# First attention of a two-layer block on one core: value products of two key blocks in halves of the columns, sums and bias on GpSimd

## The reference, cut to what matters

```
q, k, v = h @ Wq.T + bq, h @ Wk.T + bk, h @ Wv.T + bv      # h = layernorm(x), 64 columns each
weights = softmax(q @ k.T / 8, causal)
x = x + (weights @ v) @ Wo.T + bo
```

## Time and profile before

| | |
|---|---|
| median of 3 runs | 2892.86 us (2884.68 to 2895.48) |
| the profiled execution's own time | 2893.18 us |
| its span, first to last instruction | 2891.3 us |
| PE busy | 2605.1 us, 90% |
| DVE busy | 2001.3 us, 69% |
| ACT busy | 1590.3 us, 55% |
| POOL busy | 397.3 us, 14% |
| granted TensorE clock, mean | 0.959 of full speed |

### The profile page before, as it was taken

How to read it: one execution, slowest core, us unless ns; L and a number is a source line. 1 busy time by engine, 2 the same in 40 slices (tenths; PEclk the granted TensorE clock), 3 DMA queues, 4 the chain that set the end, 5 groups by cost and what they waited for, 6 DMA issues and landing times.

```text
span 2891.3 us, 57833 instructions
## 1 busy us (share of the span) xinstructions
PE 2605.1 (90%) x21618; PEld 1170.1 (40%) x21618; DVE 2001.3 (69%) x4383; ACT 1590.3 (55%) x3169; POOL 397.3 (14%) x417
## 2 busy tenths in 40 slices
PE   6798789899899899999899889999989989899996
PEld 3444333334344344443344434343344434334344
DVE  4557778776666777777675677877667577887832
ACT  2324356555545556555564556656555466666663
POOL 2322020201102011120201202020010110000011
PEclk9889799999999999999999999999999999999998
DMA  2423131211311313130221312213031131111101
GB/s 56 135 73 111 45 97 31 75 53 38 87 36 48 97 45 97 31 104 16 75 65 33 97 36 79 71 45 97 23 87 38 40 104 38 45 52 38 33 28 35
DMA packets 238692, 175.93 MB, mean 61 GB/s; under 512 B 88721, under 2 KB 238162, under 8 KB 238418
## 3 DMA queue, kind: packets, MB, share of 16 engines
q1 hardware_dynamic: 236560, 170.39, 20.8%
q10 hardware_dynamic: 1858, 1.84, 0.2%
HBM read 87.17 MB, written 84.41 MB: 59 GB/s over the span
## 4 chain that ended last, share of the span: by engine, by line
PE 57%; DVE 20%; ACT 6%; SPq 6%; issue 4%; DMA 4%; DVEq 1%; POOL 1%; POOLq 0%; ACTq 0%
DVE mx L1273 14%; PE psum L1556 12%; PE psum L1537 10%; PE psum L1510 6%; PE psum L1444 4%; SPq L754 4%; PE psum L1478 4%; ACT probs L1053 3%; DMA rest_dram<-parts 2%; PE psum L1418 2%; PE psum L1360 2%; PE psum L1574 2%; PE psum L1497 2%; DVE stats L1154 2%; PE psum L1584 2%
## 5 line engine op out<-in xcount | busy, mean ns | idle before, releaser
L1273 DVE TENSOR_REDUCE mx<-psum 128x1 f32<-128x512 f32 (+3 forms) x2560 | 1386.9, 601 | 343.5 <-PE psum L1510 169.6
L1053 ACT ACTIVATE probs<-psum 128x512 f32<-128x512 f32 (+3 forms) x2560 | 1186.3, 538 | 710.1 <-PE psum L1537 427.7
L1537 PE MATMUL psum<-qst,kst 34*128 34x512 bf16 (+7 forms) x5120 | 680.9, 353 | 58.1 <-ACT probs L1053 23.2
L1556 PE MATMUL psum<-probs,vs 128*17 128x512 f32 (+3 forms) x5120 | 607.8, 547 | 2.2 <-ACT probs L1053 1.6
L1510 PE MATMUL psum<-kst,qst 64*128 64x512 bf16 (+3 forms) x2560 | 450.4, 357 | 91.5 <-DVE mx L1273 31.1
L1537 PEld LDWEIGHTS psum<-qst,kst 64*128 64x128 bf16 (+1 forms) x5120 | 196.6, 95 | 412.7 <-DVE mx L1273 144.3
L1510 PEld LDWEIGHTS psum<-kst,qst 64*128 64x128 bf16 x2560 | 131.3, 94 | 501.0 <-ACT probs L1053 182.9
L888 POOL TENSOR_SCALAR vare<-mv 128x4 f32<-128x4 f32 x64 | 14.9, 232 | 1615.1 <-DVE mv L1157 1615.1
L1013 ACT ACTIVATE probs<-psum 128x1024 f32<-128x1024 f32 x80 | 74.6, 939 | 141.9 <-PE psum L1424 80.8
L1556 PEld LDWEIGHTS psum<-probs,vs 128*17 128x17 f32 x5120 | 86.3, 96 | 159.7 <-issue 103.8
L1516 PE MATMUL psum<-maskq,identh 64*128 64x128 bf16 x2048 | 147.8, 219 | 0.0
(11 more groups left out here) (150 smaller groups left out, 2584.2 us busy)
## 6 DMA issues: line engine op xcount, KB each, us to landing
main_dram<-parts SPq DMA_DIRECT2D x256, 128.0 KB
rest_dram<-parts SPq DMA_DIRECT2D x128, 128.0 KB
qst<-main_dram SPq DMA_DIRECT2D x128, 128.0 KB, 2.8
kst<-main_dram SPq DMA_DIRECT2D x128, 128.0 KB, 2.8
v_dram<-vst SPq DMA_DIRECT2D x64, 136.0 KB, 4.0
vs<-v_dram SPq DMA_DIRECT2D x64, 136.0 KB, 2.3
xs<-x_in SPq DMA_DIRECT2D x16, 512.0 KB, 4.0
x_dram<-xs SPq DMA_DIRECT2D x16, 512.0 KB, 3.1
```

The source lines that it names most:

```text
L1053: act.activation(probs[:, HG * (step_no(b, hg, k) % 2) + 2 * pair + odd, 0:cols], bank(PLAN.home["scores", item[:4]][odd], 0, cols), ACT.E ...
L1273: dve.tensor_reduce(mx1[:, n % 2, 2 * g + odd, i % TPC, c:c + 1], bank(PLAN.home["max", item[:5]][odd], 0, width(i, c)), AX.X, ALU.max).th ...
L1537: ins = pe.matmul(two[odd][:, 0:CH - off], kst[rows, kslot, part, pair, keys], qst[rows, qslot, part, pair, off:CH], start=(part == 0), st ...
L1556: ins = pe.matmul(bank(7, off, CH, rows=VW, row=32 * h), vtile[:, h, :], probs[:, HG * (step_no(b, hg, k) % 2) + h, 0:CH - off], start=(kb ...
```

## The change

- For q of 1 to 3, `values0` writes the even block of a pair to PSUM rows 0 to 63 and the odd block to rows 64 to 127, so the two use the left and the right half of the array's columns. For q = 0 both blocks go to rows 0 to 63, one after the other as before. The column of ones is gone; v0 has 64 columns. The planner knows it as a new mode "H", at half the time of before for q of 1 to 3.
- `copy0` copies 128 rows (64 for q = 0). `wo0` holds Wo twice, in rows 0 to 63 and 64 to 127, so that `WO0` 1 and 2 add the halves in their contraction.
- A new job `sum0` on GpSimd adds up each pair's exponentials in `sums0` (128 x 512): for a full pair two additions that wait for one another, for the first pair of q of 1 to 3 one addition of the two blocks. `exp0` of pair n now waits for `sum0` of pair n-2 too. `WO0` 0 multiplies `sums0` with a column of ones and waits for the chunk's last `sum0`, not for `copy0`.
- A new job `bias0` on GpSimd adds the bias to x, once for each chunk, after the first norm; `add0` waits for it. The bias (bo, and bv times Wo, spread over all rows with one matmul at the start) is in `boc`.
- At the start, one weight load more on SP's queue, one of 128 KB instead of 1 KB on ACT's, two small memsets and some waits fewer on GpSimd, one small multiplication on DVE.

```diff
-SWITCH = {("F", "R"): 0.31, ...}
+SWITCH = {..., ("F", "H"): 0.31, ("R", "H"): 0.15, ("C", "H"): 0.14, ("H", "C"): 0.14, ("H", "F"): 0.14, ("H", "R"): 0.14}
+    add("POOL", "bias0", c, key(0), 2.4, ("norm", (0, *c)))
...
-        add("ACT", "exp0", (*c, kp), key(0.6), 0.17 + 0.853 * size, ("scores0", (*c, kp)), ("values0", old),
+        add("ACT", "exp0", (*c, kp), key(0.6), 0.17 + 0.853 * size, ("scores0", (*c, kp)), ("values0", old), ("sum0", old),
             free=("scores0", (*c, kp)))
-        add("PE", "values0", (*c, kp), key(0.6), 1.71 * size - (0.21 if diagonal else 0), ("exp0", (*c, kp)),
-            ("v0", (b, 2 * kp // TPC)), ("values0", (*c, kp - 1) if kp else None), lat=0.1, claim="O" if kp == 0 else None, mode="F")
-    add("ACT", "copy0", c, key(), 0.5, ("values0", (*c, pairs - 1)), *[("WO0", p and (*p, n)) for n in range(3)],
+        less = P / CH if diagonal else 0.0
+        add("PE", "values0", (*c, kp), key(0.6), 0.86 * size if q else 0.86 * (2 * size - less), ("exp0", (*c, kp)),
+            ("v0", (b, 2 * kp // TPC)), ("values0", (*c, kp - 1) if kp else None), lat=0.1, claim="O" if kp == 0 else None, mode="H")
+        add("POOL", "sum0", (*c, kp), key(0), 1.2 * (2 * size - less if kp or not q else 1.0), ("exp0", (*c, kp)),
+            ("sum0", (*c, kp - 1) if kp else None), ("WO0", p and kp == 0 and (*p, 0) or None))
+    add("ACT", "copy0", c, key(), 0.5, ("values0", (*c, pairs - 1)), *[("WO0", p and (*p, n)) for n in (1, 2)],
...
-        add("PE", "WO0", (*c, n), key(), 0.3 if n == 0 else 0.86, ("copy0", c), lat=0.1, claim="P", mode="F")
+        add("PE", "WO0", (*c, n), key(), 1.0 if n == 0 else 0.86, ("copy0", c) if n else ("sum0", (*c, pairs - 1)),
+            lat=0.1, claim="P", mode="F")
...
+                elif kind == "bias0":
+                    b, q = item
+                    wt.wait_ge("ready", 1)
+                    wt.job("norm", (0, b, q))
+                    x = xs[:, q % 2, :, :]
+                    pool.tensor_tensor(x, x, boc[:, :].unsqueeze(1).broadcast_to([P, TPC, D]), ALU.add).then_inc(S["bias0"], 1)
+                elif kind == "sum0":
+                    b, q, kp = item
...
+                    if kp == 0 and q:
+                        pool.tensor_tensor(sums0[:, :], even, odd, ALU.add).then_inc(S["sum0"], 1)
+                        continue
+                    links += 1
+                    if kp == 0:
+                        pool.tensor_copy(sums0[:, :], even).then_inc(S["chain s"], 1)
+                    else:
+                        pool.tensor_tensor(sums0[:, off:CH], sums0[:, off:CH], even, ALU.add).then_inc(S["chain s"], 1)
+                    wt.wait_ge("chain s", links)
+                    pool.tensor_tensor(sums0[:, lo:CH], sums0[:, lo:CH], odd, ALU.add).then_inc(S["sum0"], 1)
...
-                        ins = pe.matmul(ps[0:DK0 + 1, lo:CH], v0[:, kb, :], probs0[:, n % 2, odd, lo - off:CH - off],
-                                        start=(kb == 0), stop=(kb == TPC * (q + 1) - 1))
+                        up, first = (odd, kp == 0) if q else (0, kb == 0)
+                        ins = pe.matmul(ps[DK0 * up:DK0 * (up + 1), lo:CH], v0[:, kb, :],
+                                        probs0[:, n % 2, odd, lo - off:CH - off], start=first,
+                                        stop=(kp == TPC * (q + 1) // 2 - 1 if q else kb == TPC - 1))
...
-                            ins = pe.matmul(ps[:, t:t + 1], osb0[:, P * t:P * (t + 1)], wo0[:, D:D + 1],
+                            ins = pe.matmul(ps[:, t:t + 1], sums0[:, P * t:P * (t + 1)], wo0[:, D:D + 1],
```

More of the change, by code:

```diff
@@ L312, in chunk_jobs @@
         else:
-            add("DVE", "add0", (*c, n), key(), 0.79, ("WO0", (*c, n)), ("rec0", c), ("norm", (0, *c)),
+            add("DVE", "add0", (*c, n), key(), 0.79, ("WO0", (*c, n)), ("rec0", c), ("bias0", c),
                 free=("WO0", (*c, n)))
@@ L892, in _ @@
                         pool.memset(kst[:, :, 1, :, :], 1.0).then_inc(done, 1)
+                elif kind == "bias0":
[3 more added lines that the diff above has]
+                    x = xs[:, q % 2, :, :]
+                    pool.tensor_tensor(x, x, boc[:, :].unsqueeze(1).broadcast_to([P, TPC, D]),
+                                       ALU.add).then_inc(S["bias0"], 1)
+                elif kind == "sum0":
+                    b, q, kp = item
+                    old = before(b, q)
+                    n = len(PAIRS0) * b + PAIR_AT[q, kp]
+                    off = span(q, 2 * kp)
+                    lo = span(q, 2 * kp + 1)
+                    even = probs0[:, n % 2, 0, 0:CH - off]
+                    odd = probs0[:, n % 2, 1, lo - off:CH - off]
+                    wt.job("exp0", item)
+                    if kp == 0:
+                        wt.job("WO0", old and (*old, 0))
+                    else:
+                        wt.job("sum0", (b, q, kp - 1))
+                    if kp == 0 and q:
+                        pool.tensor_tensor(sums0[:, :], even, odd, ALU.add).then_inc(S["sum0"], 1)
+                        continue
+                    links += 1
+                    if kp == 0:
+                        pool.tensor_copy(sums0[:, :], even).then_inc(S["chain s"], 1)
+                    else:
+                        pool.tensor_tensor(sums0[:, off:CH], sums0[:, off:CH], even, ALU.add).then_inc(S["chain s"], 1)
+                    wt.wait_ge("chain s", links)
+                    pool.tensor_tensor(sums0[:, lo:CH], sums0[:, lo:CH], odd, ALU.add).then_inc(S["sum0"], 1)
                 elif kind == "bias":
@@ L1010, in _ @@
                         wt.job("values0", (bb, *PAIRS0[m]))
+                        wt.job("sum0", (bb, *PAIRS0[m]))
                     wt.job("scores0", item)
@@ L1017, in _ @@
                     old = before(b, q)
-                    for n in range(3):
+                    for n in (1, 2):
                         wt.job("WO0", old and (*old, n))
                     wt.job("values0", (b, q, TPC * (q + 1) // 2 - 1))
-                    act.activation(osb0[:, :], home("values0", (b, q, 0))[0:DK0 + 1, :], ACT.Copy
+                    rows = slice(0, P if q else DK0)
+                    act.activation(osb0[rows, :], home("values0", (b, q, 0))[rows, :], ACT.Copy
                                    ).then_inc(S["copy0"], 1)
@@ L1217, in _ @@
                         wt.wait_ge("weights", W0)
-                        dve.tensor_tensor(wo0[DK0:DK0 + 1, 0:D], bank(7, 0, D, rows=1, row=DK0),
-                                          wo0[DK0:DK0 + 1, 0:D], ALU.add).then_inc(S["ready"], 1)
+                        dve.tensor_tensor(boc[:, :], bank(7, 0, D), boc[:, :], ALU.add).then_inc(S["ready"], 1)
                         eight_bit_weights()
@@ L1228, in _ @@
                     wt.job("rec0", (b, q))
-                    wt.job("norm", (0, b, q))
+                    wt.job("bias0", (b, q))
                     wt.job("WO0", item)
@@ L1401, in _ @@
                         wt.wait_ge("weights", W0)
-                        pe.matmul(bank(7, 0, D, rows=DK0 + 1), bvcol[:, :], wo0[0:DK0, 0:D], start=True, stop=True
+                        wt.wait_ge("spread", 1)
+                        pe.matmul(bank(7, 0, D), bvcol[:, :], wo0[0:DK0, 0:D], start=True, stop=True
                                   ).then_inc(S["apart"], 1)
```

49 lines of the change are left out of this document (28 added, 21 removed).

## The result

The changed kernel takes 2877.35 us (median of 6 runs, 2870.71 to 2883.92), the kernel before, run beside it, 2893.09 (2884.68 to 2895.48): a ratio of 0.9949 [0.9929, 0.997], 16 us or 0.5% faster. The forecast was 2854 (2832 to 2880). The side was right and the time lies in the range, but less than half of the 39 us came.

The account below looks back on a forecast made before the run. PE was taken as the only limit inside the values0 bursts, with DVE limiting some of what follows. 44 us gained - 3 (modes) - 2 (DVE) = 39, from a median of 2892.86 to 2854 us, range 2832 to 2880.

Parts of the forecast that it names:

- Products, 53 us less: values0 on PE: pairs in halves run together, a full pair falling from 1.86 to 0.98 us; 53 us less PE work.
- the 44 in the sum: Part of the 53 us of PE work expected to reach the end: 35 us in batches 1 to 3, 9 in batch 0.
- 0.88 and 0.7: Shares of saved PE work taken to reach the end: 0.88 in batches 1 to 3, 0.7 in batch 0.
- The rest on PE, ACT: WO0 contracting 128 rows instead of 65, and copy0 with 128 rows: nothing.
- The 3 us for modes: values0 no longer shares a mode with transposes and projections: 3 us lost (0 to 11).
- GpSimd paces the bursts: Rival: sums of 17.8 us against bursts of 18 to 19 us set the pace; 2878 us, chance 0.10.
- the slower rival: PE stands at WO0 0 for a sum0 behind a late root; 2934 or 2918 us, chance 0.06.
- GpSimd's work on the chain, 2 us: DVE standing still while GpSimd writes: DVE's 20% of the chain applied to 10 us, 2 us lost.
- DVE time lost: DVE work such as xn and xrk held up by more GpSimd work: 10 us of DVE time (0 to 20).
- The start, nothing (at most 1 us): One more SP load issue, fewer POOL memsets, a small DVE multiplication: nothing, at most 1 us either way.
- Order, 10 either way: New order on PE, DVE and ACT: may move time by 10 us either way, put only in the range.

Follow-up runs that it names:

- e13: Changed kernel, a pair's value products one after the other and GpSimd's new work left out; ratio 1.0059 to the kernel before; its two theories expected at most 2900 us.
- e3: Changed kernel, same order and waits, GpSimd's new work left out (sums and bias not computed); 2854.19 us, ratio 0.9879 to the kernel before.
- e2: Changed kernel with ACT's weight loads held behind memsets and the first bias0 held until DVE has made the 8-bit weights; 2867.88 us, ratio 0.9929.
- e5: e2 with batch 0's sum0 replaced by a memset of one column; 2861.23 us, ratio 0.9892 to the kernel before.
- e1: Changed kernel with ACT's weight loads issued only behind ten GpSimd memsets, as before the change; 2873.95 us, ratio 0.9949.
- e15: e2 with each addition of batch 0's sums replaced by a GpSimd power of 4 columns: queue nearly as full, hardly any data moved; 2871.19 us, ratio 0.9919.
- e14: e2 with the second chunk's load issued on SP ahead of the later weights; 2862.06 us, ratio 0.9903 to the kernel before.
- e8: Kernel before, with WO0 0 planned at 1.0 us instead of 0.3, only the order changed; 2884.45 us, ratio 0.9968.
- e12: Kernel before, with the plan's LEAD at 84 instead of 85, only the order changed; 2881.83 us, ratio 0.9955.
- e11: Changed kernel, with WO0 0 planned at 0.3 us again instead of 1.0, only the order changed; 2882.34 us, ratio 0.995.
- e4: Changed kernel in its own order, both blocks of every pair to rows 0 to 63, one after the other; 2911.21 us, ratio 1.0077.

## Why the prediction was right in sign and wrong in size

**Products, 53 us less: right.** A pair takes 1.01 us for a forecast 0.98. PE's busy time fell 47 us for a forecast 50. Without GpSimd's work the halves bring 52 us of total time (e13 to e3, some 8 either way; 46 in their traces) for the 44 in the sum. So 0.88 and 0.7 for what reaches the end were not too high; the loss stood elsewhere.

**The rest on PE, ACT: right.** `WO0` and the copies cost nothing: a 128-row copy takes 598 ns, and a matmul of `WO0` 1 or 2 with 128 rows 389 ns for 409. `exp0` waited 2.8 us for sums. The 3 us for modes weren't measured by themselves; they are in what the order costs, below.

**GpSimd paces the bursts: no.** 17.44 us of sums fit in the burst, which became 3.8 to 5.9 us shorter; e3's is only 0.2 us shorter still. Nor did PE stand at `WO0` 0 (1.3 us of idle time in all), so the slower rival didn't come. Its mechanism did, turned around: not a sum behind a late root, but a root behind sums.

**GpSimd's work on the chain, 2 us: wrong, and the largest error.** It costs 20 us (e3 against the changed kernel, some 8 either way), and by the marks nearly all of it is lost in batch 0: 19.5 us of the 21.6 between the two traces. 11 us come through batch 0's sums (e2 to e5); 4 us or so at the start, from the bias (the first value product, e1 to e2). The DVE time lost was sized about right: DVE is busy 14.5 us longer than in e3 (2032.2 for 2017.7), 6.6 of them in `xn` and 4.2 in the two instructions at the start, for an estimate of 10 (0 to 20). What failed was to give it DVE's average share of the chain, 20%. In batch 0 the norms are what PE waits for: up to 235 us the transposes of `xn` (L1403) waited 35.5 us for DVE, in the kernel before 22.8, in e3 29.7. And the in-order queue was looked at only for what a sum waits for, not for what waits behind a sum. I had counted no price for it, and by e15 it is the larger part of what batch 0's sums cost.

**The start, nothing (at most 1 us): wrong.** The first value product starts 9.0 us later (57.6 for 48.6): 4.1 from the bias additions that stretch two DVE instructions (e2 brings them back), about as much from the load (in e14, with the load at 8.7 us, the product is at 46.1). I had named both edits and priced neither by the row where POOL and DVE meet, though it is from the same stretch.

**Order, 10 either way: I had put it at zero, and its range may have been too small.** e13 pays 17 us over the kernel before (11 to 23 by its interval), of which 5.8 are there by the first `copy0` (58.3 for 52.5), with the load landing 4.3 us later. Some 11 are left for the order, though the two traces show only 4.4 of them (10.2 us apart in all). e8 and e12 show that 9 and 13 us lie between neighbouring orders.

The sum, from ratios: 17 (order and loads) - 52 (halves) + 20 (GpSimd) = -15, where the forecast had 3 - 44 + 2 = -39. That it ends at the measured -15 (0.9949) proves nothing, as the terms are differences of the same ratios. It is one path through the four corners; along the other it reads 17 + 5 - 37. The side was right because the largest term was; with an order as lucky for the kernel before as e12's, no gain would have shown. That the time lies in the range was luck: its upper end, 2880, stood there for GpSimd pacing the bursts, which didn't happen.

**Open.** Which pairs of instructions in the new order cost the 11 us wasn't found, and e13 exceeded both theories. One wait grew with the order: behind batch 0, PE's matmul at L1558 waits for ACT's `xnT` 4.5 us in the kernel before, 20.0 in e13 and 19.2 in the changed kernel. But in e11 it is 5.3 us and the ratio is the same, so it doesn't decide the time. The split of what batch 0's sums cost is read from one trace each; in the total it isn't resolved. That bytes ahead of the load delay it is argued from e1 and e14, which moved issue times, not bytes.

## What to carry to other kernels

When work moves to an idle engine, ask first what that engine already does in small pieces that others wait for: every such piece now queues behind the new work. Price the move in the stage where those pieces are on the chain (here the first batch), not by an average share. And before calling a change of half a per cent a gain in a kernel with a planned order, run two neutral variations of the plan: here they moved the time by 9 and 13 us, nearly as much as the change itself (15).

## What the runs showed of the hardware that I hadn't expected

Where GpSimd runs additions one after another, DVE gets through about one instruction between two of them: four `xn` in 5.46 us beside four additions of 1.27, and two instructions of 0.41 us took 2.45 and 2.56 beside two additions that took 5.87 together. About the same busy time on GpSimd with 4 columns an instruction (e15) stretched next to nothing: 86.2 us of `xn` for 85.6.

Float32 products with 128 rows in halves of the columns run together: 1.01 us for the four matmuls of a pair, which start in twos 0.01 us apart, and 1.86 us for the same four one block after the other (e4).
